# Two-layer cross-attention: the inverse deviation of both halves of a unit from one GpSimd power

## The reference

```python
q = einsum('bte,ef->btf', emb, Wq) + bq
k = einsum('bml,le->bme', latent, Wk) + bk
v = einsum('bml,le->bme', latent, Wv) + bv
w = softmax(einsum('bte,bme->btm', q, k) * E ** -0.5, axis=1)
x = einsum('btm,bme->bte', w, v) + emb
mu, var = mean(x, -1), var(x, -1)
return (x - mu) * rsqrt(var + 1e-6) * gamma + beta
```

## Time and profile before

| | |
|---|---|
| median of 3 runs | 1100.29 us (1098.56 to 1103.39) |
| profiled execution | 1106.36 us, its span 1104.6 us |
| busy in the span: PE, weight loads | 95%, 89% |
| DVE, ACT, POOL | 80%, 72%, 71% |
| granted PE clock over the span | 0.978 of full, 1.00 in the steady part |
| powers on POOL (L1182) | 128, 801 ns in the mean, 102.5 us |
| DVE's wait for them (before L1038) | 60.0 us in 94 waits |

### The profile page before, as it was taken

How to read it: one execution, slowest core, us unless ns; L and a number is a source line. 1 busy time by engine, 2 the same in 40 slices (tenths; PEclk the granted TensorE clock), 3 DMA queues, 4 the chain that set the end, 5 groups by cost and what they waited for, 6 DMA issues and landing times.

```text
span 1104.6 us, 26238 instructions
## 1 busy us (share of the span) xinstructions
PE 1046.1 (95%) x8392; PEld 981.9 (89%) x8392; DVE 882.5 (80%) x2561; ACT 791.7 (72%) x2033; POOL 786.5 (71%) x646
## 2 busy tenths in 40 slices
PE   4999999999999999999999999999999999999984
PEld 3889999899999999999999999999999999999873
DVE  1558888888888888888888888898888888888864
ACT  1446777777777777877777777778777777777743
POOL 0035787778777877877778777878877777778754
PEclk8899999999999999999999999999999999999986
DMA  8021101111111111111101111111011111101001
GB/s 214 38 92 46 38 26 63 63 62 61 61 46 35 41 61 61 61 61 61 44 31 47 61 61 61 61 52 32 38 61 61 61 61 61 44 32 48 18 18 34
DMA packets 19218, 60.15 MB, mean 54 GB/s; under 512 B 4064, under 2 KB 6112, under 8 KB 19184
## 3 DMA queue, kind: packets, MB, share of 16 engines
q1 hardware_dynamic: 16544, 59.71, 16.6%
q10 hardware_dynamic: 2640, 0.01, 0.2%
HBM read 45.03 MB, written 14.68 MB: 54 GB/s over the span
## 4 chain that ended last, share of the span: by engine, by line
PE 87%; DVE 4%; issue 4%; ACT 2%; DMA 2%; POOL 0%; SPq 0%; DVEq 0%; POOLq 0%; ACTq 0%
PE oq_bank L574 8%; PE oq_bank L568 8%; PE oq_bank L570 8%; PE score_bank L555 8%; PE score_bank L550 8%; PE score_bank L551 7%; PE oq_bank L526 5%; PE oq_bank L521 5%; PE oq_bank L522 5%; PE t_bank L474 4%; PE pv_bank L600 4%; PE pv_bank L605 4%; PE pv_bank L601 4%; PE t_bank L492 3%; PE oq_bank L580 2%
## 5 line engine op out<-in xcount | busy, mean ns | idle before, releaser
L757 ACT ACTIVATE probs<-scores,neg_max 125x224 f32<-125x224 f32 x384 | 180.8, 474 | 128.5 <-DVE neg_max L961 126.6
L1160 POOL TENSOR_TENSOR cn_lo<-raw,cn_hi 125x768 fp32r<-125x768 f32 x64 | 137.6, 2150 | 95.7 <-ACT cn_hi L714 94.8
L550 PE MATMUL score_bank<-qT_hi,cT_hi 128*125 128x224 f32 x768 | 196.9, 283 | 0.4 <-DVE neg_max L961 0.2
L1182 POOL TENSOR_TENSOR rstd<-ve,minus_half 112x1 f32<-112x1 f32 x128 | 102.5, 801 | 126.4 <-DVE ve L1031 125.8
L551 PE MATMUL score_bank<-qT_hi,cT_lo 128*125 128x224 f32 x768 | 188.4, 272 | 0.0
L1168 POOL TENSOR_TENSOR psum<-probs 125x672 f32<-125x672 f32 x64 | 105.0, 1640 | 76.2 <-ACT probs L766 76.2
L961 DVE CUSTOM_DVE_ANT_0 scores<-score_bank,d_row 125x224 f32<-125x224 f32 x384 | 138.3, 378 | 26.1 <-PE score_bank L555 25.9
L766 ACT ACTIVATE probs<-probs,rsum 125x224 f32<-125x224 f32 x384 | 156.0, 473 | 2.2 <-DVE rsum L969 2.2
L555 PE MATMUL score_bank<-qT_lo,cT_hi 128*125 128x224 f32 x768 | 150.2, 276 | 0.0
L550 PEld LDWEIGHTS score_bank<-qT_hi,cT_hi 128*125 128x125 f32 x768 | 144.6, 188 | 1.7 <-ACT qT_hi L745 0.6
L551 PEld LDWEIGHTS score_bank<-qT_hi,cT_lo 128*125 128x125 f32 x768 | 144.9, 189 | 0.0
(11 more groups left out here) (105 smaller groups left out, 2888.7 us busy)
## 6 DMA issues: line engine op xcount, KB each, us to landing
raw<-in_ctx_dram SPq DMA_DIRECT2D x32, 750.0 KB
x<-in_x_dram SPq DMA_DIRECT2D x32, 448.0 KB, 4.8
out_dram<-y_out SPq DMA_DIRECT2D x31, 448.0 KB, 3.3
y<-in_L_xattn_Wq_dram SPq DMA_DIRECT2D x4, 512.0 KB, 10.5
x<-in_L_xattn_Wk_dram SPq DMA_DIRECT2D x2, 512.0 KB, 9.9
x<-in_L_xattn_Wv_dram SPq DMA_DIRECT2D x2, 512.0 KB, 11.3
bv_row<-in_L_xattn_bv_dram SPq DMA_DIRECT2D x2, 256.0 KB, 6.7
gamma_row<-in_L_xattn_gamma_dram SPq DMA_DIRECT2D x2, 256.0 KB, 7.7
```

The source lines that it names most:

```text
L550: nc.tensor.matmul(o, cT_hi[:, u.slot, l, cols], qT_hi[:, l, :], start=(l == 0), stop=False)
L757: ins = act.activation(probs[0:MP, u.par, c, :], scores[0:MP, c, :], ACT.Exp, bias=neg_max[0:MP, c:c + 1], scale=-1.0, accum_out=ssum[0:MP ...
L1160: pool.tensor_tensor(cn_lo[0:MP, u.slot, :, cols], raw[0:MP, u.slot, :, cols], cn_hi[0:MP, u.slot, :, cols].bitcast(F32), ALU.subtract).th ...
```

## The change

`add_eps` works on both halves at once, with 112 x 2 values, and `inverse_deviation` too. Both `shift` operations of a unit wait for the one power. In the orders of DVE and POOL the first half's steps move to the second half's place. `minus_half` becomes two columns wide. No DMA is added or moved.

```diff
--- before.py
+++ after.py
@@ -145,7 +145,7 @@
         beta_col = sb("beta_col", [P, EC])
         ident = sb("ident", [P, P])
         ones = sb("ones", [P, 2])
-        minus_half = sb("minus_half", [P, 1])
+        minus_half = sb("minus_half", [P, TH])
 
 
         x0 = sb("x0", [P, 2, TH, E])
@@ -1024,17 +1024,17 @@
                 dve.sem_inc(wait_alone, 1)
                 dve.bn_aggr(mv[0:TP, u.par, h, :], bn[0:TP, u.par, h, :]).then_inc(mv_done, 1)
 
-            def add_eps(u, h):
-                if not u.real:
-                    return
-                dve.wait_ge(mv_done, u.n(m=2, add=h - 1))
-                dve.tensor_scalar(ve[0:TP, u.par, h:h + 1], mv[0:TP, u.par, h, 1:2], EPS, None, ALU.add).then_inc(ve_done, 1)
+            def add_eps(u):
+                if not u.real:
+                    return
+                dve.wait_ge(mv_done, u.n(m=2))
+                dve.tensor_scalar(ve[0:TP, u.par, :], mv[0:TP, u.par, :, 1], EPS, None, ALU.add).then_inc(ve_done, 1)
 
             def shift(u, h):
 
                 if not u.real:
                     return
-                dve.wait_ge(rstd_done, u.n(m=2, add=h - 1))
+                dve.wait_ge(rstd_done, u.n())
                 dve.tensor_scalar(nmr[0:TP, u.par, h:h + 1], mv[0:TP, u.par, h, 0:1], rstd[0:TP, u.par, h:h + 1], -1.0,
                                   ALU.mult, ALU.mult).then_inc(nmr_done, 1)
 
@@ -1055,7 +1055,6 @@
                         WqT_out(1)
                     q_lo(now, 1)
                     probs_lo(last, 0)
-                    shift(prev, 0)
                     add_pv(prev, 1)
                     ctxT_lo(now, 2)
                     half_moments(prev, 1)
@@ -1064,7 +1063,8 @@
                     moments(prev, 1)
                     score_max(now, 1)
                     score_max(now, 2)
-                    add_eps(prev, 1)
+                    add_eps(prev)
+                    shift(prev, 0)
                     shift(prev, 1)
                     score_max(now, 3)
                     score_max(now, 4)
@@ -1093,7 +1093,6 @@
                     q_lo(nxt, 1)
                     moments(last, 0)
                     add_pv(last, 1)
-                    add_eps(last, 0)
                     probs_lo(now, 0)
                     score_max(nxt, 0)
                     score_max(nxt, 1)
@@ -1175,11 +1173,11 @@
                     pool.wait_ge(o_ready, u.n(-1, 2, R_HALF - 1))
                 pool.tensor_tensor(psum_all[0:MP, :], psum1[0:MP, :], psum3[0:MP, 2, :], ALU.add).then_inc(psum_done, 1)
 
-            def inverse_deviation(u, h):
-                if not u.real:
-                    return
-                pool.wait_ge(ve_done, u.n(m=2, add=h - 1))
-                pool.tensor_tensor(rstd[0:TP, u.par, h:h + 1], ve[0:TP, u.par, h:h + 1], minus_half[0:TP, :],
+            def inverse_deviation(u):
+                if not u.real:
+                    return
+                pool.wait_ge(ve_done, u.n())
+                pool.tensor_tensor(rstd[0:TP, u.par, :], ve[0:TP, u.par, :], minus_half[0:TP, :],
                                    ALU.pow).then_inc(rstd_done, 1)
 
             def scale(u, h):
@@ -1214,22 +1212,20 @@
             def slot(k, j):
                 now, last, prev = Unit(k, j), Unit(k - 1, j), Unit(k - 2, j)
                 if k % 2 == 0:
-                    inverse_deviation(prev, 1)
+                    inverse_deviation(prev)
                     scale(prev, 0)
                     add_beta(prev, 0)
                     scale(prev, 1)
                     ctx_lo(now, 0)
                     sum_probs(now)
                     ctx_lo(now, 1)
-                    inverse_deviation(last, 0)
                     add_beta(prev, 1)
-                    inverse_deviation(last, 1)
+                    inverse_deviation(last)
                     scale(last, 0)
                     scale(last, 1)
                     add_beta(last, 0)
                     add_beta(last, 1)
                 else:
-                    inverse_deviation(last, 0)
                     sum_probs(now)
             slots(pool, slot)
```

## The result

The change is slower: 1168.81 us (median of 6 runs, 1168.27 to 1169.58) against 1099.99 us (6 runs, 1098.56 to 1103.39). The ratio is 1.0629, with a 95% interval of 1.0608 to 1.065. The forecast was 1143 with a range of 1112 to 1165; the direction was right, the size too small by 26 us. The profiled execution took 1169.33 us, its span 1167.5.

What follows compares the result with a forecast made beforehand. The prediction took TensorE (PE) at full clock as the bound; 1.28 us (even slot) plus 0.09 (odd slot) made 1.37 a double slot, times 31 = 42.5 us, giving 1143 us against 1100.29, with a range of 1112 to 1165.

Steps and rivals of the forecast that it cites:

- Bound and direction: Whole kernel: TensorE (PE) at full clock is the bound, and the change makes it slower, chance 0.90.
- The even slot: Even slot: late standardise(first half) delays ACT's exponentials and oT_hi, costing PE 1.28 us a double slot.
- e: POOL's power: extra time for a second value, between 0 and 0.35 us, taken as 0.18.
- the cover of 0.68 us: Even slot, pv_product: second oT_hi comes 1.49+e late, but PE stalls only 0.81+e.
- The removed instructions: DVE and POOL: one power, addition and wait fewer per unit, beside PE's work, counted as zero.
- The odd slot: Odd slot: fused power ends where the second did; xT_lo stall 0.73 us every double slot, costing 0.09.
- the three sums: POOL's odd slot: sums with one pr_lo of DVE between them, from 533.02 to 536.55, before cn_lo.
- whoever comes first goes first: DVE and POOL reading SBUF: the earlier instruction holds up the other, as with a residual held 0.94 us.
- Cascade: Odd slot rival: pr_lo waits for cn_lo, add_beta for pr_lo, power for both; up to 1 us, 1174; chance 0.07.
- Port: Rival: two-value addition waits for a POOL pass, power 0.3 us later twice a double slot; 1162 us; chance 0.06.
- Residual wins: Odd slot rival: residual starts before the second scale, so the 0.64 us stall goes; 1120 us; chance 0.17.
- The signs: Profile after: ACT idle about 2.9 us before z, double slot 33.3, DVE's power wait near 40, 64 powers of 0.54 to 0.89.

Runs made afterwards that it cites:

- e1: The change with only the first layer's units fused, the second layer keeping two powers; 1134.7 us, ratio 1.0268 to the kernel before.
- e5: The change with standardise(prev, 0) moved behind exps(now, 0) and o_hi(last, 0) in ACT's even slot; 1209.6 us, ratio 1.091 to the kernel before.
- e7: The change with the edits of e5 and e6 together; 1175.86 us, ratio 1.0605 to the kernel before.
- e11: e7 with both add_beta of the even slot's unit moved behind the odd power; 1107.59 us, ratio 0.9995 to the kernel before.
- e10: The kernel before, nothing fused, with the first half's shift behind the second half's addition in DVE's even slot; 1099.23 us, ratio 0.9916.
- e2: The change with only the second layer's units fused, the first layer as before; 1105.57 us, ratio 1.0008 to the kernel before.
- e12: The change with only DVE's half of e6: the addition of eps ahead of the second pr_lo; ratio 1.0507 to the kernel before.
- e13: The change with only POOL's half of e6: the odd slot's power ahead of add_beta; ratio 1.0496 to the kernel before.
- e4: The change with its addition of eps split into two one-value additions, power still fused; 1159.36 us, ratio 1.0495 to the kernel before.
- e6: The change with the odd slot's addition of eps ahead of DVE's second pr_lo and power ahead of add_beta; 1134.25 us, ratio 1.0237.

## Why the prediction was wrong

**Bound and direction: right.** PE bounds the kernel, at full clock, and the change costs only through PE's waits.

**The even slot: right.** Forecast 1.28 us, measured 1.24. The queue on ACT is the one described (4.47 us against 4.49), and e1 shows this term alone. Over the stretch of the table PE's third matmul of pv_product starts 1.05 us later against the spread of d (10.82 for 9.77), forecast 0.99 (0.81+e). In detail two things were off. The stall is split: 0.66 us before the transposes of z, which the forecast let begin 0.58 late (0.4+e) but counted as part of the later stall, and 0.18 in pv_product, where it had looked for a wait of 0.8 to 1.2. And the start of z came 0.47 us after the shift's (583.70 to 584.17), not 0.33. e5, e7 and e11 show that standardise's place ahead of the exponentials is the cause of both new waits: with it behind them the waits are gone, and in e11 the even part is 24.29. e10 agrees with the cover of 0.68 us that the forecast subtracted (1.49 late, 0.81 lost): 0.58 late cost nothing.

**e: right** (0.16 for 0.18). **The removed instructions:** no run shows them to bring anything, as forecast: e2 has half of them removed and a ratio of 1.0008, e11 all and 0.9995, though both move other things too.

**The odd slot: wrong, and this is the step that failed.** Forecast 0.09 us, measured 0.83. I let the three sums take 3.53 us, with one pr_lo slipped in as the second sum ended. They took 4.40 (559.82 to 564.22): the second sum itself was held, for 1.19 us, and without any hold the three take 3.13 in the kernel before (531.35 to 534.48), not the 2.93 that the working had left for them beside its 0.6. The sentence behind it, that whoever comes first goes first, is wrong as read from start times: that sum started 0.48 us before pr_lo and lost. From there the chain was late by as much: the power ends 8.88 us after the first sum's start, where the working had 8.03. That 0.85 us is the missing term. What stood behind it in the working held: from the sums' end to the power's end 4.48 us (forecast 4.50), from there to the residual 2.63 (2.7) and to xT_lo 4.20 (4.27). So the mechanism of the odd slot was right as far as it went; the sums, with the hold inside them, were the mis-sized term.

**The rivals.** Cascade (0.07, 1174 us) named the order of events that came: the second pr_lo waited for cn_lo, add_beta for pr_lo, the power for both, with e12 and e13 to show it. Its price was nearly met, but in part by luck: it looked for the time behind the sums, and there the chain took what the forecast had given it (4.48 for 4.50; what cn_lo took less, add_beta and the power took more). The excess came one step earlier, in the sums. Port (0.06) was true as well, and its price in a repeat was 0.35 us (e4), not 0.6. "Residual wins" was false; the wait for xT_lo came in 29 repeats. The working let the second pr_lo have the port for some 0.5 us after cn_lo; it began 0.76 after cn_lo's start and lasted 1.81.

**The signs.** ACT's idle time before z grew to 3.98 us (forecast 2.9), the repeat to 33.89 (33.3), DVE's wait for the power is 52.8 us (40). The 64 powers of 0.70 came as forecast.

## What to carry to other kernels

Merging two small operations makes the first wait for the second. Ask where the first result's consumer stands on an in-order queue, and what is behind it there: here 0.7 us of ACT's work moved from idle time onto the path, with the exponentials and both oT_hi behind it. Where two engines share a port, an edit that shifts one of them by half a microsecond changes which instructions meet. Such a term can't be read off as a delay: give the chain of collisions a bound from the longest passes and a real chance. And a change can be tried piece by piece: one line of this one, the late shift without the merge, won 0.8% in one slot, and 0.7% were lost when it was made in both. A gain that hangs on which of two instructions starts a few hundredths of a us earlier isn't one to build on.

## What the runs showed of the hardware

- On GpSimd the power of 112 x 1 values takes 0.54 us, of 112 x 2 values 0.70.
- VectorE's addition of a constant to 112 x 1 values in SBUF took 0.13 to 0.16 us in every run that has it, beside a GpSimd pass or not; to 112 x 2 values it took 0.16 to 1.07 in the change and e6, and at 567.55 and in e6 it ended with the pass that ran beside it.
- The order of starts in the profile doesn't tell which of the two engines gets the port. GpSimd's sum lost to a pr_lo that started 0.48 us later; a residual lost to an add_beta that started 0.07 later and won against one that started 0.11 later (e10); in e5 two residuals stood 4.25 us while scale and cn_lo followed one another.
- In e5 the granted clock was 0.63 in the 4 us behind a wait of 1.58 us, with 0.50 in the two us from 615 to 617; in e7, with as many waits of up to 1.7 us at the same place, and in the change, with waits of 1.4, it was 1.00 over the steady part.
